# Local attention tiles: turning the undivided probabilities, putting token rows out of the weighing, and dividing the outputs

## The reference, cut to what matters

```python
for l in range(DEPTH):                      # 2 layers, 8 x 128 tokens = 8 tiles each
    h = shift_token(x)
    q, k, v = split(h @ wqkv)               # 8 heads of 64
    q, k = rotary_xpos(l2norm(q) * qs, l2norm(k) * ksc)
    sim = einsum('bhwid,bhwjd->bhwij', bq, bk)      # windows of 64, keys of this and the last
    attn = softmax(where(mask, -max, sim))
    out = einsum('bhwij,bhwjd->bhwid', attn, bv)
    x = x + out @ wo
    h = layernorm(shift_token(x)) ; a, g = split(h @ w1 + b1)
    x = x + (a * gelu(g)) @ w2 + b2
```

## Time and profile before

| | us |
|---|---|
| median of 3 runs | 392.6 (392.31 to 393.21) |
| the profiled execution | 393.19 |
| its span (first to last instruction) | 391.1 |
| PE / DVE / ACT / POOL busy | 343.0 / 319.3 / 273.4 / 69.6 |
| mean granted TensorE clock | 0.983 of full speed |

### The profile page before, as it was taken

How to read it: one execution, slowest core, us unless ns; L and a number is a source line. 1 busy time by engine, 2 the same in 40 slices (tenths; PEclk the granted TensorE clock), 3 DMA queues, 4 the chain that set the end, 5 groups by cost and what they waited for, 6 DMA issues and landing times.

```text
span 391.1 us, 10135 instructions
## 1 busy us (share of the span) xinstructions
PE 343.0 (88%) x3970; PEld 244.8 (63%) x3974; DVE 319.3 (82%) x712; ACT 273.4 (70%) x703; POOL 69.6 (18%) x57
## 2 busy tenths in 40 slices
PE   2899998999977879997898889899999999997676
PEld 1388897886534345554456656576677767676565
DVE  4989979953878898978589999989898998996453
ACT  1678775664455267766556888998989898986673
POOL 2000020002053160000222223220232323221110
PEclk9999999999998999999899999999999999999889
DMA  8914483340000000000000000000000000000001
GB/s 311 385 34 77 67 105 71 58 70 3 0 0 3 1 2 0 2 2 0 2 2 2 0 2 0 3 3 0 3 0 2 3 1 2 1 3 3 0 0 55
DMA packets 18639, 12.43 MB, mean 32 GB/s; under 512 B 17056, under 2 KB 17312, under 8 KB 18336
## 3 DMA queue, kind: packets, MB, share of 16 engines
q1 hardware_dynamic: 18592, 11.78, 12.0%
HBM read 7.19 MB, written 0.52 MB: 20 GB/s over the span
## 4 chain that ended last, share of the span: by engine, by line
PE 43%; DVE 28%; ACT 15%; issue 11%; DMA 2%; ACTq 0%; DVEq 0%
PE ps L269 12%; PE ps L594 4%; PE ps L530 3%; DVE blk L1226 3%; DVE ss_floor L1236 3%; ACT PT L1577 3%; PE ps L519 2%; PE ps L638 2%; DVE Y L904 2%; PE ps L726 2%; PE ps L608 2%; PE ps L393 2%; PE ps L648 2%; PE ps L656 2%; DVE lneg L1252 2%
## 5 line engine op out<-in xcount | busy, mean ns | idle before, releaser
L1791 POOL TENSOR_TENSOR blk<-blk 128x1024 f32<-128x1024 f32 x16 | 37.7, 2358 | 167.1 <-DVE blk L1230 122.1
L594 PE MATMUL ps<-w_f,full 128*128 128x512 f32 x96 | 48.2, 619 | 0.9 <-issue 0.9
L1577 ACT ACTIVATE PT<-ps,lneg 128x128 f32<-128x128 f32 x128 | 45.0, 376 | 3.9 <-DVE lneg L1252 3.8
L1459 ACT ACTIVATE St<-ps 128x512 bf16<-128x512 f32 x32 | 19.1, 596 | 19.6 <-PE ps L269 19.6
L269 PEld LDWEIGHTS ps<-blk,st 128*128 128x128 bf16 x768 | 26.8, 98 | 3.8
L1577 ACT ACTIVATION_READ_ACCUMULATOR PT<-ps,lneg 128x1 f32 x128 | 27.7, 217 | 0.0
L269 PE MATMUL ps<-blk,rel 128*128 128x64 bf16 x768 | 27.6, 193 | 0.0
L269 PE MATMUL ps<-blk,st 128*128 128x64 bf16 x768 | 27.6, 193 | 0.0
L1634 ACT ACTIVATE PT<-ps 128x512 f32<-128x512 f32 x32 | 17.5, 595 | 12.9 <-PE ps L530 12.9
L951 DVE TENSOR_TENSOR blk<-blk,keep_b 128x1024 bf16<-128x1024 bf16 x32 | 21.9, 687 | 5.1 <-ACT blk L1446 5.0
L594 PEld LDWEIGHTS ps<-w_f,full 128*128 128x128 f32 x96 | 16.3, 192 | 13.7 <-issue 13.6
(11 more groups left out here) (237 smaller groups left out, 841.7 us busy)
## 6 DMA issues: line engine op xcount, KB each, us to landing
w_f<-f_dram SPq DMA_DIRECT2D x2, 1689.0 KB, 13.5
w_x<-l_dram SPq DMA_DIRECT2D x1, 774.0 KB, 6.0
w_f<-ffn_dram SPq DMA_DIRECT2D x1, 561.0 KB, 8.2
X<-x_dram SPq DMA_DIRECT2D x1, 512.0 KB, 3.7
ctxT<-ctxT_dram SPq DMA_DIRECT2D x1, 512.0 KB, 4.5
OT<-maskT_dram SPq DMA_DIRECT2D x1, 512.0 KB, 7.3
OT<-St SPq DMA_TRANSPOSE x31, 3.1
const<-const_dram SPq DMA_DIRECT2D x1, 388.0 KB, 6.5
```

The source lines that it names most:

```text
L594: m = mm(ps[:, c, :], hT[:, n, :], w_f[:, l, F_QKV + 512 * c:F_QKV + 512 * (c + 1)], start=True, stop=True)
L1577: e = a(S1[:, i % 2, P * k:P * (k + 1)], ps[:, 3 + c, P * j:P * (j + 1)], ACT.Exp, bias=lneg[:, i % 2, k:k + 1], accum_out=lsum[:, i % 2, ...
L1791: g_.tensor_tensor(R[:, i % 2, :], R[:, i % 2, :], T2, ALU.add).then_inc(sem("pair_sum"), 1)
```

## The change

The exponentials no longer accumulate their sums (`accum_out` and the buffer `lsum` go), and `normalise_p` goes: `turn_p` waits for the exponentials themselves. V gets a 65th column of ones per head, written once by POOL. `weigh` swaps its operands: the turned probabilities of a head (128 x 128) are stationary and V with its ones (65 columns) moves, so that the output has tokens on rows, four heads in bank 5 and four in bank 6, each with its denominator in column 64. `divide_output` on DVE takes the reciprocals of the 8 columns and multiplies the outputs into `St`; `turn_o` on PE turns the result back in four transposes to bank 5, and `take_turned_o` waits for that. The orders of PE, DVE and ACT are changed for it; in H tiles PE turns the probabilities ahead of the hidden layer, ACT copies them ahead of its gelu, and `head_root` comes behind the gelu. POOL's wait for p_norm goes.

```diff
-        VL = view(blkf, 9216, 3, LH, LD)
+        VL = view(blkf, 9216, 3, LH, LD + 1)
...
                 for c in range(2):
-                    pe.wait_ge(sem("p_norm"), 2 * i + c + 1)
+                    pe.wait_ge(sem("lexp"), 2 * i + c + 1)
...
             def weigh(i):
                 pe.wait_ge(sem("qkv_read"), i + 1)
                 pe.wait_ge(sem("p_turned"), 2 * i + 2)
+                if i == 0:
+                    pe.wait_ge(sem("v_ones"), 1)
                 for h in range(LH):
                     j, c = h // 2, h % 2
-                    m = mm(ps[64 * c:64 * (c + 1), 5, P * j:P * (j + 1)], VL[:, i % 3, h, :],
-                           P1[:, i % 2, P * (4 * c + j):P * (4 * c + j + 1)],
-                           start=(j == 0), stop=True, skip_group_check=True)
+                    m = mm(ps[:, 5 + h // 4, (LD + 1) * (h % 4):(LD + 1) * (h % 4 + 1)],
+                           P1[:, i % 2, P * (4 * c + j):P * (4 * c + j + 1)], VL[:, i % 3, h, :],
+                           start=(h % 4 == 0), stop=True, skip_group_check=True)
                 m.then_inc(sem("lo_ps"), 1)
+
+            def turn_o(i):
+                pe.wait_ge(sem("o_unit"), i + 1)
+                for j in range(4):
+                    t = tr(ps[:, 5, P * j:P * (j + 1)], St[:, i % 2, P * j:P * (j + 1)], ident)
+                t.then_inc(sem("lo_back"), 1)
...
             for i in range(4):
                 if i >= 1:
                     qkv(i + 2)
+                    turn_o(i - 1)
                 turn_qk(i + 1)
...
                 down(i, q)
+                turn_o(i - 1)
...
             def quarter_hidden_tile(i):
                 q = (i - 4) // 2
                 if i + 2 < 2 * NB:
-                    qkv(i + 2, 0, 2)
+                    qkv(i + 2)
+                turn_o(i - 1)
+                turn_qk(i + 1)
+                turn_norm(i, q)
                 project_o(i - 1)
-                if i + 2 < 2 * NB:
-                    qkv(i + 2, 2, 3)
-                turn_norm(i, q)
-                turn_qk(i + 1)
                 pe.wait_ge(sem("yT"), 7 + q)
                 score_band(i + 1)
+                turn_p(i)
                 hidden_wait(i, q)
                 for t in range(3):
                     hidden_third(q, t, 0)
-                turn_p(i)
                 score_heads(i + 1)
                 weigh(i)
...
             quarter_hidden_tile(2 * NB - 2)
             shift_tokens(2 * NB - 1, 6)
+            turn_o(2 * NB - 2)
             pe.wait_ge(sem("loT"), 2 * NB - 1)
...
             turn_norm(16, 6)
+            turn_o(2 * NB - 1)
             project_o(2 * NB - 1)
...
-            def normalise_p(i, c):
-                dve.wait_ge(sem("lexp"), 2 * i + c + 1)
-                r = lrec[:, 4 * c:4 * c + 4]
-                step(v.reciprocal(r, lsum[:, i % 2, 4 * c:4 * c + 4]))
-                settle()
-                p = S1[:, i % 2, 512 * c:512 * (c + 1)].rearrange("p (h k) -> p h k", h=4)
-                v.tensor_tensor(p, p, r.rearrange("p (h o) -> p h o", o=1).to_broadcast([P, 4, P]), ALU.mult)\
-                    .then_inc(sem("p_norm"), 1)
+            def divide_output(i):
+                dve.wait_ge(sem("lo_ps"), i + 1)
+                if i >= 2:
+                    dve.wait_ge(sem("loT"), i - 1)
+                o = ps[:, 5:7, 0:4 * (LD + 1)].rearrange("p b (h d) -> p b h d", h=4)
+                r = lrec[:, :].rearrange("p (b h) -> p b h", b=2)
+                step(v.reciprocal(r, o[:, :, :, LD]))
+                settle()
+                v.tensor_tensor(St[:, i % 2, :].rearrange("p (b h d) -> p b h d", b=2, h=4), o[:, :, :, 0:LD],
+                                r.rearrange("p b (h o) -> p b h o", o=1).to_broadcast([P, 2, 4, LD]),
+                                ALU.mult).then_inc(sem("o_unit"), 1)
...
                 largest(i)
+                divide_output(i - 1)
                 unit_norm(i + 1)
...
             def take_turned_o(i):
-                act.wait_ge(sem("lo_ps"), i + 1)
+                act.wait_ge(sem("lo_back"), i + 1)
...
                     e = a(S1[:, i % 2, P * k:P * (k + 1)], ps[:, 3 + c, P * j:P * (j + 1)], ACT.Exp,
-                          bias=lneg[:, i % 2, k:k + 1], accum_out=lsum[:, i % 2, k:k + 1])
+                          bias=lneg[:, i % 2, k:k + 1])
...
             for i in range(4, 2 * NB, 2):
                 q, more = (i - 4) // 2, i + 2 < 2 * NB
-                take_turned_o(i - 1)
                 exponential_half(i, 0)
                 if more:
                     square(i + 2)
+                take_turned_o(i - 1)
                 exponential_half(i, 1)
                 take_quarter_norm(q)
+                take_turned_qk(i + 1)
                 if more:
                     take_v(i + 2)
-                take_turned_qk(i + 1)
+                take_turned_p(i)
                 if not more:
                     break
-                head_root(i + 2)
                 nc.scalar.preload_act_table(ACT.Gelu)
                 take_gelu(q)
-                take_turned_p(i)
                 nc.scalar.preload_act_table_set(roots)
+                head_root(i + 2)
 
                 i = i + 1
-                exponential(i)
+                exponential_half(i, 0)
+                take_turned_o(i - 1)
+                exponential_half(i, 1)
                 square(i + 2)
-                take_turned_o(i - 1)
...
             def sum_pairs(i):
                 pool.wait_ge(sem("rotated"), i + 1)
-                if i >= 6 and i % 2 == 0:
-                    pool.wait_ge(sem("p_norm"), 2 * (i - 2) + 2)
                 g_.tensor_tensor(R[:, i % 2, :], R[:, i % 2, :], T2, ALU.add).then_inc(sem("pair_sum"), 1)
 
+            pool.wait_ge(sem("scores1"), G * NB)
+            g_.memset(VL[:, :, :, LD:LD + 1], 1.0).then_inc(sem("v_ones"), 1)
```

More of the change, by code:

```diff
@@ L181, in build @@
         lr = sb("lr", [2 * LH])
-        lsum = sb("lsum", [2, LH])
         lrec = sb("lrec", [LH])
@@ L1316, in _ @@
                     normalise(6, X, Z, "z_in", 4, NB)
-                normalise_p(i, 0)
-                normalise_p(i, 1)
                 rotate(i + 2)
@@ L1353, in _ @@
             largest(2 * NB - 1)
-            normalise_p(2 * NB - 1, 0)
-            normalise_p(2 * NB - 1, 1)
+            divide_output(2 * NB - 2)
             quarter_moments(6)
@@ L1358, in _ @@
             quarter_rows(6)
+            divide_output(2 * NB - 1)
             add_output(2 * NB - 1)
@@ L1662, in _ @@
             for i in range(4):
-                if i >= 1:
-                    take_turned_o(i - 1)
                 if i == 1:
@@ L1668, in _ @@
                 square(i + 2)
+                if i >= 1:
+                    take_turned_o(i - 1)
                 take_turned_qk(i + 1)
@@ L1713, in _ @@
                 head_root(i + 2)
-            take_turned_p(2 * NB - 2)
             exponential_half(2 * NB - 1, 0)
```

## The result

The kernel after takes 418.1 us (median of 4 runs, 417.8 to 421.8) against 392.9 before: a ratio of 1.066, 95% interval 1.061 to 1.072. The profiled execution took 418.3 us, its span 416.2.

What follows compares the result with a forecast made beforehand. PE was taken to bound the tile pairs and DVE the plain tiles. Plain tiles +2.5, pairs +18.0, tile 14 +2.0 and the rest of the end -1.3 made +21.2 us, hence 414 us, range 398 to 427.

Steps and rivals of the forecast that it cites:

- Weighing: Weighing on PE: weight loads pace the 16 records at 0.11 us each, 1.76 us, +0.74 a tile.
- Both ends of the range of that term: Weighing block: 0.9 us if paced by the product (chance 0.15), 2.6 us if load and product are serial (0.13).
- The walk of the pairs: Five H and D pairs stepped through with all waits: 25.85 us a pair against 22.1, +18.0 in sum.
- The four waits: PE stalls in a pair: 0.85 (keys turned) and 0.55 (turn_p) in H, 0.75 (next z) and 0.92 (band) in D.
- Relief for ACT and DVE: In the pairs, lighter ACT and DVE buy nothing in D, and in H only where PE waits.
- the later expectation of 0.8 us a tile: Theory of a later run, kernel before without sums and division: about 0.8 us less in each of three plain tiles.
- Tile 0: First local tile: no output to turn, and earlier probabilities (0.7 us) pay for its longer weigh.
- The end: Tile 14 +2.0 us; tile 15 shorter (6.7 against 9.4), +1.4 after the last weigh, net -1.3.
- if it falls so again over a longer weigh: Tile 15: if the granted clock falls again as in the 0.70 stretch, the net is +1.6 us instead of -1.3.
- The sum: Whole kernel: +2.5 + 18.0 + 2.0 - 1.3 = +21.2 us, giving 414 us.
- nothing overlapped: Weighing with load and product serial: 16 x 0.16 = 2.6 us, +1.6 a tile; as a rival 427 us, chance 0.13.

Runs made afterwards that it cites:

- the two changed sizes: Two runs on the kernel after, in the weighing: 33 instead of 65 moving columns, 421.4 us; 64 instead of 128 stationary columns, 410.1 us.
- the run without a way back: Kernel after without dividing the output and turning it back, ACT copying bank 5 as the weighing leaves it: 401.0 us, ratio 1.020.
- Order alone: Kernel after with the output copy later in D, and turn back and copy earlier in H and plain tiles: 406.3 us, ratio 1.036.

## Why the prediction was right, point by point

**Weighing.** 0.11 us a record was taken, 0.115 measured; the block 1.76 against 1.84. Both ends of the range of that term are refuted by the two changed sizes. By the Trainium skill, page "TensorE: Matmul & The Clock Gate", section "Packing small matmuls — row/col tiling", loads overlap products only where row groups differ; 16 records with 195 ns loads and 275 ns products in 1.84 us, all 128 rows in use, and hardly less (1.80) with half the columns moving, disagree with that, and the measurement decides. The same page's "LDWEIGHTS (loading the stationary operand)" gives the columns over 1.2 in ns, 107 for 128: this case comes near it, with 0.115 us a record at 128 columns; at 64 it has 1.08/16 = 0.068 where that gives 53 ns.

**The walk of the pairs.** The four waits came where they were put: 0.85 predicted and 0.78 measured (L607), 0.55 and 0.40 (L647), 0.75 and 0.73 (L577), 0.92 and 0.76 (the band). H was 13.35 and came out at 13.47, D 12.5 and 12.80; ACT's wait in D was to be "some 3 us" and is 3.07. The difference of 0.3 in D is small spacings: 0.07 up to the band, 0.10 in project_o, 0.04 in turn_p and 0.09 in the weighing. Half the cause of the first wait was missed, ACT's square in front of the copy, as the run without a way back showed. By sum the pairs are 0.9 us over: the first cost 0.8 less than the 3.7 taken, the next three 0.4 more each, the fifth 0.4 more.

**Relief for ACT and DVE.** That it would buy nothing in the pairs held (0.17 us of 22.13). For the plain tiles, where DVE bounds, the later expectation of 0.8 us a tile was low; 1.2 was measured, which touches no term of the prediction.

**Tile 0** was put at nothing and cost 0.5 us: its weighing is 0.8 longer and the earlier probabilities paid for only part.

**The end** is the term that was mis-sized: -1.3 + 2.0 = +0.7 forecast for tile 14 and what follows, +4.9 measured. The prediction named the case ("if it falls so again over a longer weigh") but priced only tile 15 with it, +1.6 instead of -1.3, and took the other value. The clock fell in three places: in tile 14, in the projection and last weighing of tile 15, and from the last project_o through the down projection behind it. With it held at 1.00, the forecast's own numbers come out within 0.3 us each.

**The sum.** +21.2 forecast, +25.1 between the two profiled spans: +0.9 in the pairs, +0.7 in tile 0 and the plain tiles, +4.2 at the end, and -1.9 in code that is the same in both. That last term is luck: without it the forecast would have been 5.8 us off, not 3.9. Two readings of the prediction are slips without effect: 8.98 us is the length of the third plain tile, in which DVE was busy 8.34, and nothing overlapped would be 16 x 0.18 by its own two costs, not 16 x 0.16.

## What to carry to other kernels

When an engine is full, count the new work on it first, and for f32 products on all 128 rows with few moving columns count by the stationary side: swapping the operands of a small product turned 64 loaded columns into 128 and cost 0.8 us a tile although fewer columns moved. It holds for all 128 rows only: the scores load 128 columns of 64 rows and take 1.09/16 = 0.068 us a record, with heads in alternate row halves; why was not tried. A chain of small hand-overs inserted into queues in order is best priced by walking one period with all its waits; where it says that an instruction must wait, everything behind it in its queue waits too. Order alone gave back 12 of the 25 us. A tile that is near its bound on several engines at once gives nothing for relief on one and loses at once for a delay on another (D: 0.17 us back, 0.72 lost).

## What the runs showed of the hardware that was not expected

PE's granted clock fell to 0.50, the lower of its two levels, after quite short stretches with waits (0.50 from 397.75 to 404.00): in the kernel after, tile 14 begins with 2.94 us in which PE was busy 0.81 at full clock, and the next 3.32 us had a mean clock of 0.62. Filled with matmuls that nobody reads, the same places ran at 1.00, and the fillers paid in both kernels (3.6 us after, 1.9 before). The untouched first 200 us go with the clock too: the five profiles that reached tile 2's qkv before 200.0 us had a mean of 1.00 up to there, the five that reached it after 201.4 us had 0.98 or 0.99. Which of its waits decides that was not tried. Weight loads of f32 with 128 columns on all rows follow each other every 0.113 to 0.115 us with 33 or with 65 columns moving.
